# Another place for the weighted-sum groups of a quad in the attention's order: pv1 behind pv0, pv3 behind pv2

## The reference

```python
q = (x @ q_w + q_b).reshape(Bx, Tx, NH, HD).transpose(0, 2, 1, 3)
kv = (x @ kv_w + kv_b).reshape(Bx, Tx, 2, NH, HD).transpose(2, 0, 3, 1, 4)
k, v = (kv[0], kv[1])
att = jnp.einsum('bhqd,bhkd->bhqk', q, k) * (1.0 / np.sqrt(HD))
att = att + build_alibi_bias(NH, Tx)[None]
att = jnp.where(causal[None, None], att, -jnp.inf)
att = jax.nn.softmax(att, axis=-1)
y = jnp.einsum('bhqk,bhkd->bhqd', att, v)
y = y.transpose(0, 2, 1, 3).reshape(Bx, Tx, Cx)
return y @ o_w + o_b
```

## Time and profile before

| what | us |
|---|---|
| median of 3 runs | 1394.97 (1391.97 to 1395.21) |
| the profiled execution | 1394.25 |
| its span | 1392.5 |
| busy in the span: PE | 1182.7 (85%) |
| busy: DVE | 854.2 (61%) |
| busy: ACT | 774.3 (56%) |
| busy: POOL | 604.3 (43%) |

### The profile page before, as it was taken

One profiled execution on the slowest core, in us unless ns is written; L12 is line 12 of the kernel. 1 busy time (PEld: TensorE's weight loads), 2 busy tenths in 40 slices (PEclk: granted clock), 3 DMA queues, 4 the chain that ended last, 5 costly groups with the idle time before them and its releaser, 6 DMA issues. The chain is left out here.

```text
span 1392.5 us, 30174 instructions
## 1 busy us (share of the span) xinstructions
PE 1182.7 (85%) x9378; PEld 849.7 (61%) x9444; DVE 854.2 (61%) x2156; ACT 774.3 (56%) x1658; POOL 604.3 (43%) x1064
## 2 busy tenths in 40 slices
PE   0368999999999999999999755997999989998874
PEld 0134545554555545554555334987999989998874
DVE  1287787877788787878787226454333245663665
ACT  0106666666666666666666722565666656665442
POOL 0004444444344444444344523777710055551687
PEclk9979999999999999999999976998999989999998
DMA  6123322332323322332222106222322123332222
GB/s 136 63 94 105 108 99 80 101 106 93 92 91 111 101 82 91 110 102 96 81 93 61 35 10 175 85 70 85 110 72 58 54 82 104 105 104 76 72 85 73
DMA packets 141320, 123.62 MB, mean 89 GB/s; under 512 B 18937, under 2 KB 127673, under 8 KB 140986
## 3 DMA queue, kind: packets, MB, share of 16 engines
q1 hardware_dynamic: 125954, 97.42, 23.0%
q0 software_dynamic: 8192, 16.79, 4.0%
q10 hardware_dynamic: 7064, 8.00, 2.5%
HBM read 73.14 MB, written 44.04 MB: 84 GB/s over the span
## 5 line engine op out<-in xcount | busy, mean ns | idle before, releaser
L515 ACT ACTIVATE probs<-scores 128x512 f32<-128x512 f32 x640 | 363.7, 594 | 185.3 <-PE scores L431 176.8
L550 POOL TENSOR_SCALAR_AFFINE_SELECT probs<-probs 128x256 f32<-128x256 f32 (+1 forms) x640 | 235.2, 378 | 342.2 <-ACT probs L515 337.4
L413 PE MATMUL maxed<-kstack,qstack 96*128 96x512 bf16 (+3 forms) x1024 | 273.4, 308 | 35.1 <-DMA kstack<-parts 30.5
L973 DVE TENSOR_TENSOR e_hid<-e_gate,e_up_ps 128x352 f32<-128x352 f32 x208 | 108.1, 520 | 216.4 <-ACT e_gate L1231 190.5
L431 PE MATMUL scores<-qstack,kstack 128*128 128x384 bf16 (+3 forms) x960 | 213.6, 295 | 17.3 <-ACT probs L515 14.0
L681 DVE TENSOR_REDUCE maxA<-maxed 128x4 f32<-128x512 f32 x256 | 175.2, 684 | 79.2 <-PE maxed L415 78.7
L413 PEld LDWEIGHTS maxed<-kstack,qstack 96*128 96x128 bf16 x1024 | 101.5, 99 | 160.9 <-issue 58.2
L415 PE MATMUL maxed<-causal,identb 128*128 128x128 bf16 x1024 | 196.0, 223 | 0.0
L447 PE MATMUL pv<-probs,vaug 128*32 128x512 f32 (+3 forms) x2048 | 191.2, 446 | 0.1
L1154 PE MATMUL e_gate_ps<-e_w_in,e_xT 128*128 (+1 forms) x624 | 160.7, 367 | 23.5 <-DVE e_xT L978 22.4
L681 DVE TENSOR_REDUCE maxB<-maxed 128x4 f32<-128x512 f32 x256 | 173.9, 679 | 6.3 <-PE maxed L415 6.3
(11 more groups left out here) (159 smaller groups left out, 1720.9 us busy)
## 6 DMA issues: line engine op xcount, KB each, us to landing
qstack<-parts SPq DMA_DIRECT2D x192, 96.0 KB
kstack<-parts SPq DMA_DIRECT2D x64, 288.0 KB
parts<-parts SPq DMA_DIRECT2D x16, 768.0 KB, 4.7
x_sorted<-zeros SPq DMA_DIRECT2D x32, 288.0 KB, 4.4
e_xs<-x_sorted SPq DMA_DIRECT2D x144, 64.0 KB
y_sorted<-e_raw_down SPq DMA_DIRECT2D x144, 64.0 KB, 1.9
xin<-in_x SPq DMA_DIRECT2D x16, 256.0 KB, 13.2
xres<-in_x SPq DMA_DIRECT2D x16, 256.0 KB, 13.1
```

The source lines that it names most:

```text
L413: pe.matmul(bank[:, col:col + (i + 1) * P], q[0:MAX_ROW, h, i * P:(i + 1) * P], ks[0:MAX_ROW, h, 0:(i + 1) * P], start=True, stop=False)
L515: act.activation(probs[g % 2][:, u * T:(u + 1) * T], scores[(UNITS * g + u) % SB][:], ACT.Exp).then_inc(S["exp_done"], 1)
L550: pool.affine_select(out=view, in_=view, compare_op=ALU.is_ge, fill=0.0, base=0, pattern=pattern, channel_multiplier=-1).then_inc(S["maske ...
L973: dve.tensor_tensor(hid[k][:, 0:F], gate[k][:], up_ps[k][:, 0:F], ALU.mult).then_inc(S["hid_done"], 1)
```

## The change

One string. pv1 stood behind unit4 and now stands behind pv0, ahead of unit2; pv3 stood behind unit7 and now stands behind pv2, ahead of unit7.

```diff
--- before.py
+++ after.py
@@ -120,7 +120,7 @@
 
 def plan(g):
 
-    score = "unit0 unit1 pv0 unit2 unit3 unit4 pv1 unit5 unit6 pv2 unit7 pv3 unit8 unit9".split()
+    score = "unit0 unit1 pv0 pv1 unit2 unit3 unit4 unit5 unit6 pv2 pv3 unit7 unit8 unit9".split()
     maxes = [f"max{MAX_AT[g] + n}" for n in range(10)]
     jobs = list(JOBS[g])
     keyed = []
```

## The result

The changed kernel takes 1428.33 us (median of 4 runs, 1424.7 to 1429.62) against 1394.51 us before (4 runs): the ratio is 1.0242, with a 95% interval of 1.0218 to 1.0265. That is 34 us, 2.4% slower, where the prediction said 1424 and 2.1%.

A forecast was written before the change was run, and what follows sets the result against it. The prediction took TensorE's instruction stream plus its waits as the bound. Its terms, 9.8 + 13.5 + 4.2 + 2 = 29.5 us on 1394.25, gave 1424 us, about 2.1% slower; range 1409 to 1433.

The forecast's parts named there:

- What bounds it: Attention: TensorE's instruction stream sets the pace, and each microsecond that it newly waits is added to the time.
- Term 1: Third quad: o starts 0.65 us later, x1t's wait grows from 1.12 to 1.77 us; 15 sequences, 9.8 us.
- term 3: Second quad: unit4 comes 0.78 us behind unit2's start and waits about 0.3 us; 14 sequences, 4.2 us.
- Term 2: First quad: q's copy goes ahead of unit2's exponential, unit4 waits, k starts 1.04 us late; 13 sequences, 13.5 us.
- is the one that ends last there today: First quad: the chain from k through k_whole and k_rest to the next quad's unit1 ends last, so 1.04 us arrive.
- The later waits: End of the first quad: TensorE stands still longer again at unit9 and at unit1 of the second quad; no size each.
- Term 4: Last sequence, without max banks: ScalarE paces it and idles longer with pv1 behind pv0; 2 us in all.
- The pairs: Max banks part most pairs, 9 of 128 are adjacent; true pairs everywhere could return up to 128 x 0.24 = 31 us.

The follow-up runs named there:

- third_quad: The kernel before, with only pv1 of the third quad moved behind max32, ahead of unit2, so that o comes later: 1.01 times before, +15.4 us.
- real_pairs: The changed kernel with pv1 right behind pv0 and pv3 right behind pv2 in every quad, max bank behind the pair: 1.0143 times before, +20.8 us.
- y1_behind: The changed kernel with job y1 of the second quad put back behind unit2: 1.0216 times before, +32.2 us, period 47.17 us.
- act_q_behind: The changed kernel, but on ScalarE alone the copy of q's high part stands behind unit2's exponential again: 1.0145 times before, +23.3 us.
- no_waits: The kernel before with jobs and units reordered in the first, third and fourth quads to remove named waits, no pair moved: 0.9903 times before, -14.1 us.
- qr_early: The order of no_waits with job qr right behind unit5 in the first quad, where it stood behind pv2: 0.9854 times before, -23.1 us.
- no_waits_pairs: The order of no_waits with pv0 pv1 adjacent in the first, second and fourth quads and pv2 pv3 in all: 0.9901 times before, -15.9 us.

## Why the prediction was right

- **What bounds it.** Right: TensorE's stream plus its waits is the period, and a delay of o came through whole: 0.89 us for 0.87 in third_quad.
- **Term 1, job o, and term 3, unit4.** From unit1 of the second quad to x1t the prediction adds 0.65 + 0.3 = 0.95 us, and 0.98 are measured. The step behind term 1, that x1t hangs on o, is shown: 6.53 us from o to x1t in the kernels before, changed, third_quad and real_pairs, wherever o stands. That x1t's wait would be 1.77 was slightly off (1.65); the missing 0.12 must stand elsewhere on the way. y1_behind gives 0.21 for term 3 alone, not 0.3.
- **Term 2, q's copy.** 1.04 us predicted, 1.09 measured (26.30 - 25.21). The wait at unit4 was predicted as 1.03 us and is 0.88; k, said to come 1.04 us late, comes 1.15 late. The later waits, named without a size, are 0.70 at unit9 and 0.30 at unit1. act_q_behind shows the cause: one copy's place on ScalarE is 0.75 of it. The step that says the chain from k by k_whole and k_rest to unit1 "is the one that ends last there today" holds for this change: k_whole comes 1.09 us later, and k_rest follows it by 3.66 us in the kernels before and changed and by 3.67 in act_q_behind. What ties the two is VectorE's list, which has no idle time between them. The step does not say that a second chain ends only 0.11 us earlier, which no_waits shows, nor that k_rest's 1.33 us could be shortened, which qr_early shows.
- **Term 4, the last sequence.** Mis-sized: 2 us were added, and the last two intervals together grew by 0.53 (35.78 + 26.92 against 34.50 + 27.67), of which o's 0.65 are term 1. So it is about zero. That real pairs gave back what ScalarE's idling cost would explain it, but no run separates the two.
- **What was not in the sum.** The clock: four periods of the profiled execution are 0.9 to 1.2 us too long, 4.0 in all, less the 0.36 by which the eleventh is longer before too, so 3.6 to 3.7. And the stretch behind the last x1t is 2.3 us shorter than before's (the last x1t is 32.7 us late, the span 30.4 longer); no run explains it, and the traces of the experiments differ there by up to 10.5 us. In all: 2.57 us by the first x1t, 12 x 2.07, 1.08 for the period behind them, 0.53 for the last two and 3.7 for the clock make 32.7, less 2.3. So there is some luck in how near 1424 comes to the profiled 1424.7: the 2 us too many of term 4 and the 2.3 at the end stand against the missing clock. The median lies 4 us above the profiled execution.
- **The pairs.** Right: the max banks between them leave the changed kernel without what a pair saves, and the price of 0.24 us was measured as 0.23.

## What to carry to other kernels

When several engines follow one merged order, moving a block on the busiest of them also moves copies and jobs against each other on the others; read each engine's new order, and ask of each job that comes later whether the chain behind it already ends last. A pair that is not adjacent saves nothing, and where it is, the saving counts only if no such chain ends last behind it. An order is improved at the producer that starts the late chain (o, q's copy and qr here), not at the place where the wait shows; and before a producer is moved, look which link would end last next.

## What the runs showed of the hardware

**In the steady part of the attention TensorE's clock fell only behind an idle time of 1.6 us or more, and not behind each of them.** In the table, 0 of 12 periods are long with steady waits at x1t from 0.24 to 1.12 us (72 periods in six kernels), 3 to 5 of 12 with 1.60 to 1.66, and 8 of 12 with 1.89. The changed kernel's windows behind two such waits, with the granted clock in the third column from the right:

```profile
420.00:422.00 2.00, 2.00 (x12) 1.62 (x11) 0.86 (x3) 1.08 (x2) 0.22 (x1) 0.50 0.19 74
...
468.00:470.00 2.00, 1.68 (x14) 1.38 (x15) 1.79 (x4) 1.30 (x3) 0.61 (x2) 1.00 0.19 78
```

```profile
419.69 1.09 PE L346 MATMUL misc<-ident,x_tiles 128*128 128x128 f32 x4 [1.65 <-DVE x_tiles L667]
```

Behind the wait of 1.65 us at 419.69 the granted clock is 0.50 for the stretch 420 to 422, its lower level of 1.2 GHz, and x1t takes 1.09 us in place of 0.63; one period later, behind the same wait (468 to 470), it stays at 1.00. Each fall costs 0.85 to 1.0 us. The one long period of qr_early (46.59 us) belongs to it too: its wait at x1t is 0.24 us, but that period holds a wait of 1.87 us for a transfer, which no other of these traces has, and pv0 behind it takes 1.93 us in place of 1.06:

```profile
180.87 0.39 PE L410 MATMUL maxed<-kstack,qstack 96*128 96x512 bf16 x1 [1.87 <-DMA kstack<-parts]
...
182.54 1.93 PE L444 MATMUL pv<-probs,vaug 128*32 128x512 f32 x8
```

The length of one wait does not decide it. In the changed kernel the clock stayed up behind the longest wait of the twelve periods (1.93 us, the twelfth x1t). In the lead-out of no_waits_pairs, where waits follow one another, it fell behind the fourth in a row of 0.68 to 0.81 us, with a granted clock of 0.82 from 802 to 803 us and 0.50 behind that; a transpose of `yraw` took 0.98 us there, and the one before it 0.66:

```profile
802.46 0.98 PE L343 MATMUL misc<-ident,yraw 128*128 128x128 f32 x4 [0.68 <-DVE ynorm L643]
```

This suggests that the idle time around a wait counts too, but why the clock falls after some waits and not after others stays open; no kernel here varied the work around a wait of fixed length.

**VectorE's subtraction and GpSimd's.** The same instruction of VectorE with two SBUF inputs takes 1.33 us beside GpSimd's subtraction and 0.74 us when the latter is nearly over. The Trainium skill (GPSIMD Engine Reference, Specifications) states the contention; the runs show its price, some 0.6 us (medians of 1328 and 742 ns), and qr_early that it can sit on the chain that ends last.
